# Two small side computations leave TensorE in a graph-layer kernel: squares folded into a turned summand, inverse norms spread along rows through DRAM

## What is computed

```python
z_l, z_g, v = h @ W_lang.T, h @ W_grav.T, h @ W_V.T
zn  = z_l / max(norm(z_l), EPS)
A_l = max(zn @ zn.T, 0) * not_eye
sq  = sum(z_g * z_g)                       # one number per row
d2  = max(sq_i + sq_j - 2 * z_g @ z_g.T, 0)
A_g = exp(-d2 / (2 * sigma**2)) * not_eye
K   = w_l * row_stochastic(A_l * mask) + (1 - w_l) * row_stochastic(A_g * mask)
out = layernorm(h + (K @ v) @ W_O.T)
```

## Time and profile before

| | us |
|---|---|
| median of 3 runs | 957.14 |
| profiled execution | 958.09 |
| its span, first to last instruction | 956.4 |
| mean granted TensorE clock | 0.991 |
| PE busy | 915.4 (96%) |
| DVE busy | 750.3 (78%) |
| ACT busy | 535.0 (56%) |
| POOL busy | 306.9 (32%) |

### The profile page before, as it was taken

How to read it: one execution, slowest core, us unless ns; L and a number is a source line. 1 busy time by engine, 2 the same in 40 slices (tenths; PEclk the granted TensorE clock), 3 DMA queues, 4 the chain that set the end, 5 groups by cost and what they waited for, 6 DMA issues and landing times.

```text
span 956.4 us, 18776 instructions
## 1 busy us (share of the span) xinstructions
PE 915.4 (96%) x6800; PEld 537.2 (56%) x6800; DVE 750.3 (78%) x1696; ACT 535.0 (56%) x956; POOL 306.9 (32%) x390
## 2 busy tenths in 40 slices
PE   3999999989999999999999999999999999999993
PEld 3777796555555555556464646555555555555451
DVE  5787398768888888888787888888887878786766
ACT  6787656675646455555546464646373646463531
POOL 3777372235040404040505050505050504041410
PEclk9999999999999999999999999999999999999997
DMA  6454230110413232313141413232222323121211
GB/s 266 176 200 155 87 90 1 45 45 6 96 57 88 64 81 66 89 53 104 38 119 29 116 33 109 42 101 48 94 55 87 58 84 71 73 57 45 56 46 44
DMA packets 101704, 75.84 MB, mean 79 GB/s; under 512 B 80544, under 2 KB 80672, under 8 KB 99616
## 3 DMA queue, kind: packets, MB, share of 16 engines
q1 hardware_dynamic: 101664, 75.32, 27.1%
HBM read 38.86 MB, written 16.78 MB: 58 GB/s over the span
## 4 chain that ended last, share of the span: by engine, by line
issue 50%; PE 19%; POOL 13%; DVE 11%; ACT 4%; DMA 1%; POOLq 1%; DVEq 0%; ACTq 0%
POOL arena L438 6%; PE bank L530 2%; PE bank L264 2%; PE bank L266 2%; PE bank L265 2%; POOL arena L443 2%; PE bank L537 2%; PE bank L536 2%; POOL arena L477 2%; ACT arena L1149 1%; POOL rn_parts L460 1%; POOL part_rest L458 1%; DVE stats L1636 1%; PE bank L500 1%; PE pair L264 1%
## 5 line engine op out<-in xcount | busy, mean ns | idle before, releaser
L264 PE MATMUL bank<-arena 128*128 128x512 f16 (+2 forms) x1056 | 293.8, 302 | 6.1 <-DVE arena L1690 2.0
L266 PE MATMUL bank<-arena 128*128 128x512 f16 (+2 forms) x1056 | 293.3, 301 | 0.0
L265 PE MATMUL bank<-arena 128*128 128x512 f16 (+2 forms) x1056 | 293.3, 301 | 0.0
L264 PE MATMUL pair<-arena 128*128 128x512 f16 (+1 forms) x400 | 151.2, 378 | 0.0
L265 PE MATMUL pair<-arena 128*128 128x512 f16 (+1 forms) x400 | 150.9, 378 | 0.0
L266 PE MATMUL pair<-arena 128*128 128x512 f16 (+1 forms) x400 | 150.8, 378 | 0.0
L264 PEld LDWEIGHTS bank<-arena 128*128 128x128 f16 x1056 | 103.6, 98 | 67.4 <-DVE arena L1690 4.3
L266 PEld LDWEIGHTS bank<-arena 128*128 128x128 f16 x1056 | 103.8, 98 | 63.5 <-issue 0.8
L265 PEld LDWEIGHTS bank<-arena 128*128 128x128 f16 x1056 | 103.8, 98 | 54.7 <-issue 0.3
L460 POOL TENSOR_TENSOR sq_parts<-cf,zero 128x4 bf16<-128x4 f32 x16 | 3.4, 210 | 397.2 <-DVE cf L1739 397.2
L438 POOL TENSOR_TENSOR arena<-arena 128x512 f32<-128x512 f32 x64 | 81.1, 1268 | 60.0 <-ACT arena L1059 59.6
(11 more groups left out here) (337 smaller groups left out, 1930.0 us busy)
## 6 DMA issues: line engine op xcount, KB each, us to landing
arena<-in_x SPq DMA_DIRECT2D x33, 1024.0 KB, 5.5
out_dram<-arena SPq DMA_DIRECT2D x15, 1024.0 KB, 4.3
arena<-arena SPq DMA_TRANSPOSE x75, 3.2
arena<-in_w_grav_t SPq DMA_DIRECT2D x1, 1024.0 KB, 7.4
arena<-in_w_lang_t SPq DMA_DIRECT2D x1, 1024.0 KB, 5.2
arena<-in_w_v SPq DMA_DIRECT2D x1, 1024.0 KB, 8.0
arena<-in_w_o_t SPq DMA_DIRECT2D x1, 1024.0 KB, 9.2
out_dram<-arena SPq DMA_DIRECT2D x4, 256.0 KB, 2.4
```

Of the source, the lines that this page charges most:

```text
L264: pe.matmul(dst, ah, bh, start=start, stop=False)
L265: pe.matmul(dst, ah, bl, start=False, stop=False)
L266: return pe.matmul(dst, al, bh, start=False, stop=stop)
```

## The change

**Squares.** DVE takes the diagonal of T (not of T + T') from bank 5 right after `half_products(1)`, and writes `dev`, T minus its own diagonal element in each row. High and low parts are made of `dev` instead of T, so that the turned summand brings the column term with it. The scales `HALF_DOWN` and `HK` and the factor 2 in the norms follow from that.

**Inverse norms.** SP writes them to DRAM (128 partitions, 16 bytes each) and reads them back broadcast to 128 partitions, 2 KB each. POOL multiplies that with the mask (`rn_mask`), reading it with a step of four elements. DVE then makes `a_l` in one operation from bank 4. `t_l`, `part`, `part_rows`, `along_rows`, both small ACT copies and their constants are gone.

**Order.** PE does `mix_nodes(g+1, 0)` ahead of both `add_turned`. `residual(1)` goes ahead of the new POOL product, `residual(2)` behind it. On DVE the four pieces of `x_low` are spread out, `first_stats(2)` and `(3)` go behind the row factors of `a_l`, and `k_mix` goes ahead of `first_factors(1)`; on ACT the copy of K goes ahead of `first_norm(2)`.

```diff
+M_DOWN, HALF_DOWN = 2.0 ** -16, 2.0 ** -6
 ALPHA = 1.0 / (X_UP * W_UP * XW_DOWN * A_UP)
...
 tile_at = iter(range(88 * KIB, 110 * KIB, 2 * KIB))
-diag_l, diag_g, t_l, a_l, e_g, a_g, k_g, k_mix = (
-    at(next(tile_at), [GB, P]) for _ in range(8))
+diag_l, diag_g, rn_mask, a_l, e_g, a_g, k_g, k_mix, dev, rn_row = (
+    at(next(tile_at), [GB, P]) for _ in range(10))
...
+    def inverses_along(g):
+        sp.wait_ge(s["r_ready"], g + 1)
+        sp.dma_start(rn_dram, nl[:, 5, :]).then_inc(s["rn_out"], 16)
+        sp.wait_ge(s["rn_out"], g * 16 + 16)
+        sp.dma_start(rn_row.rearrange("p b n -> p (b n)"),
+                     rn_dram.rearrange("(o n) b -> o (n b)", o=1).broadcast_to([P, N4])).then_inc(s["rn_in"], 16)
+
...
+    inverses_along(0)
...
+        inverses_along(g)
...
-
     def body(g, slot, has_next):
-        pool.wait_ge(s["dg_ready"], g * 2 + 2)
-        part(g, cf[:, 1, :], sq_parts, s["sq_rows_ps"], (s["part_steps"], 0), s["sq_parted"])
         if has_next:
             residual(g + 1, 1 - slot, 0)
-        pool.wait_ge(s["r_ready"], g + 1)
-        pool.wait_ge(s["sq_parted"], g + 1)
-        part(g, nl[:, 5, :], rn_parts, s["rn_rows_ps"], (s["part_steps"], 4), s["rn_parted"])
+            residual(g + 1, 1 - slot, 1)
+        pool.wait_ge(s["rn_in"], g * 16 + 16)
+        pool.tensor_tensor(rn_mask, rn_row.rearrange("p b n -> p (b n)").rearrange("p (n b) -> p b n", b=GB),
+                           for_items(mask[:]), ALU.mult).then_inc(s["rm_ready"], 1)
         if has_next:
-            residual(g + 1, 1 - slot, 1)
             residual(g + 1, 1 - slot, 2)
...
@@ -804,25 +764,14 @@
         else:
             between = lambda b, ks=range(KB): values(g, slot, b, True, ks)
             pe.wait_ge(s["w_l_ready"], 5)
+        between(0)
         pe.wait_ge(s["half_g_l_ready"], g + 1)
         add_turned(1, s["gg_ps"])
-        between(0)
         pe.wait_ge(s["half_l_l_ready"], g + 1)
         add_turned(0, s["gl_ps"])
-        between(1, range(0, 1))
-
-        pe.wait_ge(s["sq_parted"], g + 1)
-        part_rows(0, sq_parts, s["sq_rows_ps"])
-        between(1, range(1, 3))
-        squares_along(g)
-        between(1, range(3, KB))
+        between(1)
         between(2)
-
-        pe.wait_ge(s["rn_parted"], g + 1)
-        part_rows(P, rn_parts, s["rn_rows_ps"])
-        between(3, range(0, 2))
-        inverses_along(g)
-        between(3, range(2, KB))
+        between(3)
         if has_next:
...
@@ -1187,20 +1135,16 @@
         if has_second and not has_previous:
             x_high(g + 2, slot, loads, range(GB))
-        half_high(1, s["half_g_ps"], s["half_g_h_ready"])
-        half_high(0, s["half_l_ps"], s["half_l_h_ready"])
+        half_high(1, dev, s["dev_ready"], s["half_g_h_ready"])
+        half_high(0, bank[4][:].rearrange("p (b n) -> p b n", b=GB), s["half_l_ps"], s["half_l_h_ready"])
         if has_next:
             add_bias(g + 1, 0)
-        act.wait_ge(s["sq_rows_ps"], g + 1)
-        wait(act, s["sq_ps"], g)
-        act.activation(sq_rows[:], bank[6][0:GB * PARTS, 0:P], ACT.Copy,
-                       scale=-0.5).then_inc(s["sq_rows_ready"], 1)
...
@@ -1220,9 +1161,9 @@
         v_high(0)
         if has_next:
             first_roots(g + 1, 1)
-            first_norm(g + 1, 1 - slot, 2)
             act.wait_ge(s["k_ready"], g + 1)
             act.activation(k_parts[:, 0:GB, :], k_mix, ACT.Copy, scale=K_UP).then_inc(s["kT_h_ready"], 1)
+            first_norm(g + 1, 1 - slot, 2)
             first_norm(g + 1, 1 - slot, 3)
         v_high(1)
...
     dve.wait_ge(cs, 6)
-    dve.tensor_scalar(c1(HK), c1(KAPPA), -0.5, None, ALU.mult).then_inc(cs, 1)
+    dve.tensor_scalar(c1(HK), c1(KAPPA), -1.0, None, ALU.mult).then_inc(cs, 1)
...
@@ -1716,7 +1656,7 @@
         if not has_previous:
             xw_low(g + 1, 0)
         if has_second and has_previous:
-            x_low(g + 2, slot, range(0, HALF))
+            x_low(g + 2, slot, range(0, 1))
         z_low(0, s["zl_h_ready"], s["zl_l_ready"], 0)
         if has_previous:
             second_factors(g - 1)
@@ -1728,26 +1668,29 @@
             second_norm(3)
         z_low(0, s["zl_h_ready"], s["zl_l_ready"], 2)
         z_low(0, s["zl_h_ready"], s["zl_l_ready"], 3)
-        if has_second:
-            x_low(g + 2, slot, range(HALF, GB) if has_previous else range(GB))
-
-        half_low(1, s["half_g_h_ready"], s["half_g_l_ready"])
-        dve.wait_ge(s["gg_ps"], g + 1)
+
+
+        dve.wait_ge(s["half_g_ps"], g + 1)
         dve.tensor_tensor(diag_g, gg, for_items(ident[:]), ALU.mult).then_inc(s["dg_ready"], 1)
-        half_low(0, s["half_l_h_ready"], s["half_l_l_ready"])
         dve.wait_ge(s["dg_ready"], g * 2 + 1)
         dve.tensor_reduce(cf[:, 1, :], diag_g, AX.X, ALU.add).then_inc(s["dg_ready"], 1)
         dve.wait_ge(s["dg_ready"], g * 2 + 2)
+        dve.tensor_tensor(dev, gg, per_item(cf[:, 1, :]), ALU.subtract).then_inc(s["dev_ready"], 1)
         dve.tensor_scalar(cf[:, 0, :], cf[:, 1, :], c1(HK), None, ALU.mult).then_inc(s["hk_ready"], 1)
-
-        dve.wait_ge(s["gl_ps"], g + 1)
+        if has_second:
+            x_low(g + 2, slot, range(1 if has_previous else 0, 2))
+        dve.wait_ge(s["half_g_h_ready"], g + 1)
+        half_low(1, dev, s["half_g_l_ready"])
+
+        dve.wait_ge(s["half_l_h_ready"], g + 1)
         dve.tensor_tensor(diag_l, gl, for_items(ident[:]), ALU.mult).then_inc(s["nl_steps"], 1)
+        half_low(0, gl, s["half_l_l_ready"])
         dve.wait_ge(s["nl_steps"], g * 2 + 1)
         dve.tensor_reduce(nl[:, 5, :], diag_l, AX.X, ALU.add).then_inc(s["nl_steps"], 1)
         dve.wait_ge(s["nl_steps"], g * 2 + 2)
-        dve.tensor_scalar(nl[:, 0, :], nl[:, 5, :], 1e-18, None, ALU.max).then_inc(s["nl_in"], 1)
-
-        dve.scalar_tensor_tensor(t_l, gl, 0.0, for_items(mask[:]), ALU.max, ALU.mult).then_inc(gs, 1)
+        dve.tensor_scalar(nl[:, 0, :], nl[:, 5, :], 2.0, 1e-18, ALU.mult, ALU.max).then_inc(s["nl_in"], 1)
+        if has_second:
+            x_low(g + 2, slot, range(HALF, HALF + 1))
         newton(g, nl, s["nl_exp"], s["nl_steps2"], nl[:, 3, :], 3).then_inc(s["nl_steps2"], 1)
         dve.wait_ge(s["nl_steps2"], g * 3 + 3)
...
@@ -1773,15 +1716,15 @@
         if has_next:
             first_stats(g + 1, 1)
             first_moments(g + 1, 0)
-            first_stats(g + 1, 2)
+        if has_second:
+            x_low(g + 2, slot, range(HALF + 1, GB))
+        if has_next:
             first_factors(g + 1, 0)
-        dve.wait_ge(s["rm_ps"], g + 1)
-        dve.tensor_tensor(a_l, t_l, bank[7][:].rearrange("p (b n) -> p b n", b=GB), ALU.mult).then_inc(gs, 1)
-        dve.wait_ge(gs, g * 4 + 4)
+        dve.wait_ge(s["gl_ps"], g + 1)
+        dve.wait_ge(s["rm_ready"], g + 1)
+        dve.scalar_tensor_tensor(a_l, gl, 0.0, rn_mask, ALU.max, ALU.mult).then_inc(gs, 1)
+        dve.wait_ge(gs, g * 3 + 3)
         dve.tensor_reduce(cf[:, 2, :], a_l, AX.X, ALU.add).then_inc(fs, 1)
-        if has_next:
-            first_stats(g + 1, 3)
-            first_moments(g + 1, 1)
         dve.wait_ge(fs, g * 6 + 3)
         dve.tensor_tensor(cf[:, 4, :], cf[:, 2, :], nl[:, 5, :], ALU.mult).then_inc(fs, 1)
         dve.wait_ge(fs, g * 6 + 4)
@@ -1792,15 +1735,18 @@
         dve.scalar_tensor_tensor(cf[:, 3, :], cf[:, 5, :], c1(W_L), nl[:, 5, :], ALU.mult,
                                  ALU.mult).then_inc(s["cl_ready"], 1)
         if has_next:
-            first_factors(g + 1, 1)
-        v_low(0)
-
+            first_stats(g + 1, 2)
+            first_stats(g + 1, 3)
+            first_moments(g + 1, 1)
         dve.wait_ge(s["cl_ready"], g + 1)
         dve.wait_ge(s["kg_ready"], g + 1)
         for b in range(GB):
             last = dve.scalar_tensor_tensor(k_mix[:, b, :], a_l[:, b, :], cf[:, 3, b:b + 1], k_g[:, b, :],
                                             ALU.mult, ALU.add)
         last.then_inc(s["k_ready"], 1)
+        if has_next:
+            first_factors(g + 1, 1)
+        v_low(0)
...
```

76 lines of the change are left out of this document (15 added, 61 removed).

## The result

| | before | after |
|---|---|---|
| median, us | 957.0 | 979.36 |
| range of four runs | 956.38 to 957.51 | 977.39 to 981.63 |
| span of the profiled execution | 956.4 | 979.9 |
| mean granted TensorE clock | 0.991 | 0.987 |

The change makes the kernel slower by 2.3% (ratio 1.0226, 95% interval 1.0213 to 1.0239). The forecast was 967, with its own range to 977 and the whole to 982: the direction and the places were right, the size was not, +22 us where +10 was forecast.

The account below looks back on a forecast made before the run. PE was taken as the bound, other engines close behind. Period 46.91 to 47.7 us: fourteen periods +11.2, last group -1.1, in all +10, so median 957.1 becomes 967; own range 961 to 977, 8-in-10 range 932 to 982.

Parts of the forecast that it names:

- The squares: Turned squares on DVE and ACT hide behind half_products(0) and mix_nodes(0), by 1.8 and 0.9 us: cost nothing.
- What PE saves, and 45.3 us if all else followed: PE: 1.33 us a group around dropped row matmuls, 0.3 between the half_products; period from 46.91 to 45.3 us.
- Rival A: PE stays the bound: POOL doesn't hold up DVE's short steps, or the DMAs land suitably; 934 us, chance 0.21.
- The two DMAs: Inverse norms' write to DRAM and broadcast read: 2.4 us each, bound 3.2 each; 4.9 us with semaphores.
- The product: POOL's multiplication of the broadcast norms with the mask: 1.27 us, between 1.04 and 2.5.
- The wait placed in POOL's list: residual(2), k_g, residual(3) queue behind the landing without a hole; earlier, Newton's steps on DVE end at 555.0, not 554.2.
- three tiny ones: DVE's three small steps between a_l's reduction and K's factor: from 564.8 to 565.4, 0.6 us.
- the moments blocked as well: DVE: a landing shortly before x_low lets POOL in first and blocks the moments too: +1 us a group.
- The sum: Period 47.7 us, +0.8; fourteen full periods +11.2, last group -1.1: in all +10 us, 968 us profiled.
- The last but one group: It has no projection; PE waits for K there before and after at nearly the same time: 0 us.
- C: The stepped read in POOL's product costs half as much again: +0.63 us a group, 976 us; chance 0.13.
- D: DRAM round trip slower than any row: from 3.3 us a DMA on; 985 us middle, 995 worst; chance 0.10.

Follow-up runs that it names:

- squares_only: The kernel before with only the squares half of the change, inverse norms still by bf16 parts and matmuls on PE: 945.6 us, ratio 0.9866.
- psum_pool_first: The kernel after with DVE and ACT order of before, tiny steps' operands in PSUM, POOL's k_g and residual(2) ahead of the product: 937.7 us.
- psum_factor: The kernel after with the tiny DVE results between a_l's row sums and K's factor kept in PSUM instead of SBUF: 966.3 us.
- trip_twice: psum_pool_first with the broadcast read done twice in a row, each waited for: 996.0 us.
- pool_first: The kernel after with POOL's k_g and residual(2) moved ahead of the product that waits for the broadcast: 977.4 us.

## Why the prediction was right and wrong

**The squares**: right. DVE starts `diag_g` at 605.40, ACT's high part of `dev` at 607.6 (forecast 607.5 in this frame: the forecast's 546.55 is 605.40 here), and PE does its first `add_turned` at 610.58 without a wait. squares_only shows it by itself.

**What PE saves, and 45.3 us if all else followed**: right, but in psum_pool_first (45.30 in the usual group), not in the kernel after. Rival A (934) named its condition, that POOL doesn't hold up DVE's short steps; with that made true, and POOL's order with it, 937.7 was measured.

**The two DMAs**: 4.9 us forecast, 5.6 measured in this group (613.68 to about 619.3); in the mean of the fourteen the product starts 0.5 us later than forecast. The write was shorter (1.4), the broadcast longer: 3.9 in the median where 2.4 was taken from a store of as many bytes. The broadcast is outside the bound of 3.2 given to each, the sum of the two inside.

**The product**: 1.53 where 1.27 was taken.

**The wait placed in POOL's list**: right, a hole-free list behind it, and Newton's first step blocked (1.00).

**The step that failed is one term: the "three tiny ones" at 0.6 us** between `a_l`'s reduction and L1735. In the group at 605, L1729 starts at 622.45 and L1733 ends at 624.59: 2.1 us; in the group at 861 the same three take 2.2. So it is in twelve of the fourteen groups. In the forecast they fell into a hole of 0.45 us between `residual(3)` (to 564.65) and `low_h(0)` (from 565.1). In the group at 861 POOL's `residual(3)` ended 0.4 us later than forecast and DVE's reduction 0.7 us earlier, and the hole was gone: `low_h` starts as `residual(3)` ends.

Against DVE's start on `diag_g`, in the mean of the fourteen groups: `a_l` starts 0.6 us earlier than forecast (16.2 for 16.85), because `first_factors(0)` is blocked by 1.5 us and not 2.6, which more than makes up for the later landing (0.5) and the longer product (0.26). From there to the end of L1735 it takes 4.3 us and not 2.8, and 1.3 of these 1.5 are the three steps. So `k_mix` ends 0.85 us later than forecast (23.3 for 22.45), and the mean period is 0.76 longer. That the mean period, 48.46, left the range of 47.3 to 48.4 by so little is in part luck: two errors of over 1 us stood against each other. The range itself was also drawn too narrow for its own terms: the moments blocked as well were put at +1, which alone gives 48.7.

psum_factor agrees: with these steps out of POOL's reach a group is 1.1 us shorter. It frees L1735 too (0.22 for 0.85 us), whose wait the forecast had, so it doesn't price the three steps by themselves.

**The sum.** Over the forecast's 47.7 a group: nine groups +8.1 us together, one group +2.0 for the clock, four +0.6. **The last but one group**, costed at nothing, gave +2.6 (45.91 to 48.47); that step was wrong by itself. K wasn't there "at nearly the same time": PE waits 4.23 us for its turn where it waited 1.85. From the end of `half_products(0)` the wait ends after 26.0 us where it was 25.0 (read from the first `add_turned`, with the 2.6 us of the 12 matmuls that the kernel after does ahead of it), so 1.0 of the 2.6 us are K's. The other 1.6 come behind the wait: from its end to the same point of the next group PE takes 22.5 us instead of 20.9, and in the two stretches of 2 us from 924 on the granted clock is 0.65 and 0.50, where the kernel before shows 1.00 throughout. The end gained 0.5 instead of 1.1. With the first group's -0.7 this is 13.2 us above a forecast of +10.1, against 23.5 by which the spans differ.

**Rivals.** C (the step half as dear again) did not hold: a fifth. D held for one DMA of two, 3.9 us and 1.4 instead of 4 and 4, and trip_twice shows that its rate was about right: 2.9 us a group for 3.1 of delay.

What stays open: how much of the kernel after's loss `first_factors` makes in its own order. pool_first gained only 2 us there, where with the order of before the same move gained 49 and 37; in those two it took away the wait of `first_stats(2)` for `residual(2)`, which the changed order doesn't have.

## What to carry to other kernels

When a chain of tiny VectorE steps runs beside a GpSimd list without a hole, charge every step of it up to the end of the GpSimd operation beside it; whether it falls into a gap of half a microsecond isn't to be forecast. Where PSUM has room, put the intermediate operands there: with POOL's order and that of before on DVE and ACT this took the blocked time from 3.7 to 0.05 us a group, and a kernel that lost 1.8% became one that gains 2.1%. Where only some of the steps are out of the way, the wait can move to the next chain of tiny steps, as in pool_first. And before a wait for a transfer is put into an engine's list, move everything that doesn't need it ahead, on that engine and on the ones that wait for it.
